# Whose job is the last sum of a batch: one GpSimd addition per batch dropped, and its two terms added by VectorE in PSUM

## The reference

```python
u  = causal_conv4(xc) + conv_b            # (512 tokens, 512 channels)
dt = clip(sigmoid(u @ dt_w.T + dt_b), 1e-4, 1.0)
Bm, Cm = u @ B_w.T, u @ C_w.T             # (512 tokens, 16 states)
for t in tokens:                          # a scan over the tokens
    state = exp(clip(dt[t] * A, -5, 5)) * state + dt[t] * Bm[t] * u[t] + 1e-6
    y[t]  = sum(state * Cm[t], over the 16 states) + D * u[t]
out = (y * silu(z)) @ out_w.T
```

## Time and profile before

| | before |
|---|---|
| median of 3 runs | 1909.05 us (1909.0 to 1915.85) |
| the profiled execution's own time | 1916.34 us |
| its span | 1914.3 us |
| state-space layer with its scans | from about 570 to 1625 us of the span |
| busy over the span | PE 83%, DVE 59%, ACT 51%, POOL 54% |
| mean granted TensorE clock | 0.895 of full speed |

### The profile page before, as it was taken

How to read it: one execution, slowest core, us unless ns; L and a number is a source line. 1 busy time by engine, 2 the same in 40 slices (tenths; PEclk the granted TensorE clock), 3 DMA queues, 4 the chain that set the end, 5 groups by cost and what they waited for, 6 DMA issues and landing times.

```text
span 1914.3 us, 21817 instructions
## 1 busy us (share of the span) xinstructions
PE 1580.1 (83%) x6438; PEld 979.1 (51%) x6439; DVE 1131.5 (59%) x1730; ACT 967.6 (51%) x1749; POOL 1032.0 (54%) x354
## 2 busy tenths in 40 slices
PE   2899686999689979889889799799798684807997
PEld 1565663666335545445445455454455453804665
DVE  4665520444517677786786876777867877323443
ACT  1222111333138867777677777677767773102332
POOL 2010024222107978788888788788787897052222
PEclk9999768999899989989899899799899687658999
DMA  9700114211201111011011110111111110522110
GB/s 330 259 0 0 34 52 126 60 57 51 94 12 28 39 28 36 32 30 38 29 33 34 29 38 30 28 39 31 31 34 34 34 34 23 198 75 68 59 58 25
DMA packets 67889, 108.61 MB, mean 57 GB/s; under 512 B 8730, under 2 KB 37279, under 8 KB 67553
## 3 DMA queue, kind: packets, MB, share of 16 engines
q1 hardware_dynamic: 54240, 76.65, 13.1%
q0 software_dynamic: 9344, 27.31, 3.8%
q10 hardware_dynamic: 4224, 3.67, 0.6%
HBM read 80.04 MB, written 29.39 MB: 57 GB/s over the span
## 4 chain that ended last, share of the span: by engine, by line
PE 66%; DVE 11%; issue 10%; ACT 5%; POOL 5%; DMA 1%; ACTq 1%; SPq 1%; DVEq 0%; POOLq 0%
PE ps L1029 13%; PE ps L1248 10%; PE ps L1189 8%; PE ps L1172 7%; PE ps L1353 6%; PE ps L1279 4%; DVE arena L985 4%; PE ps L1054 3%; POOL arena L371 3%; PE ps L1332 3%; PE ps L1224 3%; PE ps L1315 2%; POOL arena L378 2%; DVE ps L933 2%; PE ps L1045 2%
## 5 line engine op out<-in xcount | busy, mean ns | idle before, releaser
L985 DVE TENSOR_TENSOR_SCAN arena<-arena,ps 128x512 f32<-128x512 f32 x512 | 613.1, 1213 | 255.2 <-PE ps L1029 236.5
L371 POOL TENSOR_TENSOR arena<-arena 128x2048 f32<-128x2048 f32 x128 | 580.3, 4540 | 235.8 <-DVE arena L985 235.1
L1029 PE MATMUL ps<-cst,arena 128*128 128x128 f32 x2836 | 481.4, 300 | 171.1 <-DVE arena L985 55.0
L1029 PEld LDWEIGHTS ps<-cst,arena 128*128 128x128 f32 x2836 | 377.5, 155 | 460.8 <-issue 267.0
L558 ACT ACTIVATE arena<-arena,a_neg 128x512 f32<-128x512 f32 x512 | 366.4, 716 | 138.2 <-DVE arena L985 137.2
L569 ACT ACTIVATE arena<-arena,m_bt 128x512 f32<-128x512 f32 x512 | 363.2, 709 | 29.3 <-PE ps L1029 28.0
L378 POOL TENSOR_TENSOR arena<-arena 128x2048 f32<-128x2048 f32 x64 | 290.5, 4539 | 5.0
L1248 PE MATMUL ps<-arena,tapw 128*128 128x512 f32 x512 | 256.7, 614 | 1.6 <-ACT arena L526 0.9
L478 ACT ACTIVATE arena<-ps,b1t 128x128 f32<-128x128 f32 x312 | 89.2, 368 | 167.4 <-PE ps L1029 167.4
L346 POOL DMA_INDIRECT sorted_rows<-x,pos x64 | 62.3, 974 | 199.1 <-DVE tile_e L814 180.1
L1189 PE MATMUL ps<-arena 128*128 x624 | 151.3, 385 | 7.4 <-ACT arena L478 2.9
(11 more groups left out here) (132 smaller groups left out, 1465.2 us busy)
## 6 DMA issues: line engine op xcount, KB each, us to landing
arena<-c_rows SPq DMA_DIRECT2D x128, 256.0 KB, 3.2
arena<-in_W SPq DMA_DIRECT2D x32, 512.0 KB, 10.5
sorted_rows<-arena POOLq DMA_DIRECT2D x2, 5070.0 KB, 36.0
arena<-sorted_rows SPq DMA_DIRECT2D x78, 130.0 KB, 2.1
x<-in_x SPq DMA_DIRECT2D x8, 512.0 KB, 10.6
arena<-in_conv SPq DMA_DIRECT2D x4, 1024.0 KB, 6.3
x<-residual SPq DMA_DIRECT2D x8, 512.0 KB, 7.6
arena<-in_b SPq DMA_DIRECT2D x2, 1024.0 KB, 11.7
```

Of the source, the lines that this page charges most:

```text
L371: g.tensor_tensor(h, h, m_c[i % RC].unsqueeze(1).to_broadcast([P, KI, SEQ]), ALU.mult)\
L985: v.tensor_tensor_scan(out=h[:, k, :], data0=m_a[g % RA], data1=ps[2 + g % 2][:, :], initial=0.0, op0=ALU.mult, op1=ALU.add).then_inc(S("m ...
L1029: return t.transpose(bank, src[:, k * P:(k + 1) * P], ident)
```

## The change

For the last pair of each batch (pairs 7, 15, ..., 63) GpSimd makes the two products and no sum. VectorE adds both states to PSUM itself: first the odd one (`m_ho`), then, after a wait for its own addition (`m_odd`), the even one (`m_he`), since both write the same bank. It does so in slots 8 to 11 of the next batch and not in 12 to 15; the wait is on the products (`m_cp`) in place of the sum. `summed(pair)` gives the count of `m_q` that now stands for a pair. The scans of the second pair of a batch no longer wait for `m_q`, since VectorE itself has read `m_ho` earlier in its queue.

```diff
+def summed(pair):
+    return pair + 1 - (pair + 1) // PAIRS
...
             for pair in range(BATCH * NS // 2):
                 c_product(2 * pair)
                 c_product(2 * pair + 1)
+                if pair % PAIRS == PAIRS - 1:
+                    continue
                 g.wait_ge(S("m_cp"), 2 * pair + 2)
                 g.tensor_tensor(m_he[pair % 3], m_he[pair % 3], m_ho[pair % 2], ALU.add).then_inc(S("m_q"), 1)
...
-                v.wait_ge(S("m_q"), pair + 1)
+                last = pair % PAIRS == PAIRS - 1
+                if last:
+                    v.wait_ge(S("m_cp"), 2 * pair + 2)
+                else:
+                    v.wait_ge(S("m_q"), summed(pair))
...
+                if last:
+                    v.tensor_tensor(ps[4 + k][:, :], ps[4 + k][:, :], m_ho[pair % 2][:, k, :], ALU.add)\
+                        .then_inc(S("m_odd"), 1)
+                    v.wait_ge(S("m_odd"), KI * b + k + 1)
                 v.tensor_tensor(ps[4 + k][:, :], ps[4 + k][:, :], m_he[pair % 3][:, k, :], ALU.add)\
                     .then_inc(S("m_add"), 1)
...
-                if n % 2 and pair >= 2:
-                    v.wait_ge(S("m_q"), pair - 1)
+                if n % 2 and pair >= 2 and (pair - 2) % PAIRS < PAIRS - 1:
+                    v.wait_ge(S("m_q"), summed(pair - 2))
...
                         turn = (SLOTS * b + q) // KI - 5
-                        if turn >= 0 and turn % 2 == 0 and turn // 2 % PAIRS >= PE_PAIRS:
+                        if turn >= 0 and turn % 2 == 0 and PE_PAIRS <= turn // 2 % PAIRS < PAIRS - 1:
                             m_add(turn // 2, q % KI)
+                        if turn > 0 and turn % 2 and (turn + 1) // 2 % PAIRS == PAIRS - 1:
+                            m_add((turn + 1) // 2, q % KI)
...
             def m_nsum(pair, k):
-                t.wait_ge(S("m_q"), pair + 1)
+                t.wait_ge(S("m_q"), summed(pair))
```

## The result

The changed kernel is slower: 1932.39 us median of 5 runs (1927.23 to 1934.84) beside 1912.53 us for the kernel before in the same session (1909.0 to 1915.85), a ratio of 1.0104 with a 95% interval of 1.0081 to 1.0126, or 19.9 us. The sum in the prediction was 12.9 us, and 1932.4 lies just above its range of 1915 to 1930. The profiled execution took 1934.84 us with a span of 1932.8, 18.5 us above that of the kernel before.

What follows compares the result with a forecast made beforehand. Each batch was taken as one chain through VectorE's scans and TensorE, with GpSimd hardly waited for. 12.0 + 2.6 - 1.75 = 12.9 us, added to the median 1909.05, gave 1922 us; own range 1915 to 1930, 8 in 10 for 1911 to 1931.

Steps and rivals of the forecast that it cites:

- The sum in the prediction: Whole kernel: 12.0 us for batches 1 to 6 plus 2.6 for batch 7 less 1.75 in the tail, 12.9 us slower.
- Slots 8 to 16: From scan 8 to scan 16 of a batch: VectorE's added additions make it 15.62 us against 13.61.
- the dependent step: VectorE, slots 8 to 11: the even addition starts 0.69 us after the odd one it waits for, bounds 0.58 and 0.80.
- The hand-over to TensorE in slots 18 to 20: Transposes of slots 18 and 20 wait for VectorE's scans, so scan 16's delay passes into TensorE's queue and every later slot.
- the clock rival: Slots 11 to 20: TensorE's granted clock falls there, 8 us a batch more, 1970 us in all; 9 in 100.
- the missing sum gives nothing in the batches: Inside the batches: GpSimd, without the last pair's sum, waits for VectorE's scans one product later; gain nothing.
- each batch is one chain, and nothing in it runs to a clock of its own: Whole batch: a delay of scan 16 passes through slots 18 and 20 into every later slot.
- the 2.0 us: Batches 1 to 6: scan 16 and the rest of the batch come 2.0 us later each, 12.0 us together.
- a scatter of up to 4 us around the sum: Seven batches: distances of 132.56 and 133.56 us, mixed in another share, move the time by up to 4 us.
- the tail: End of the last batch: from GpSimd's last product to the finals 5.2 us in place of 6.95, a gain of 1.75.
- all of batch 7's delay reaches this product: Last batch: the full 2.6 us reach GpSimd's product at 1566.59, which waited 1.01 us for a scan.

Runs made afterwards that it cites:

- pool_only: The changed kernel without the odd addition of each batch's last pair, the even one in slots 12 to 15: 1907.49 us beside 1914.49 for the kernel before.
- thrice: The kernel before and the changed one, transposes made three times over in slots 0 to 7 and 50 to 63: 1952.06 and 1961.18 us.
- split: The changed kernel with the even addition moved back to slots 12 to 15, the odd one in 8 to 11: 1938.23 us beside 1914.49 for the kernel before.
- the pads: The kernel before plus one (256, 400 columns) or two linked (220, 320) PSUM multiplications in each of slots 8 to 11: ratios 1.0016, 1.0062, 1.0088, 1.0087.
- pad2x320: The kernel before plus two linked 320-column VectorE multiplications on PSUM in each of slots 8 to 11, batches 1 to 7: ratio 1.0087.
- pad256: The kernel before plus one 256-column VectorE multiplication on PSUM in each of slots 8 to 11, batches 1 to 7: ratio 1.0016.
- dve_only: The kernel before, all GpSimd sums kept, VectorE adding the odd state and then the sum, linked, in slots 8 to 11: 1923.0 us beside 1914.49.
- delay1: The kernel before plus one 8-column SBUF-to-SBUF VectorE operation behind the scan in each of slots 8 to 11, batches 1 to 7: ratio 1.0259.
- delay3: The kernel before plus three linked 8-column SBUF-to-SBUF VectorE operations behind the scan in each of slots 8 to 11, batches 1 to 7: ratio 1.0474.

## Why the prediction was right and wrong

*Right: where the time goes and how much it is there.* Slots 8 to 16 were forecast at 15.62 us and took 15.61 in each batch (that it fits to a hundredth is luck: 9.78 for 9.72 up to slot 12, 5.83 for 5.90 behind it); the dependent step was 0.70 us for the 0.69 taken from the earlier trace rows. The rule of the Trainium skill ("VectorE: DVE Perf Modes", "The DRAIN you can't avoid"), by which the step would have been 0.58, did not hold for it. The hand-over to TensorE in slots 18 to 20 came as in the earlier trace rows, slots 16 to 48 took the same 65.5 us, and the granted clock stayed at 1.00 in slots 8 to 19 (1121.6 to 1142.0), which rules out the clock rival in the place that it named:

```profile
1121.60:1142.00 20.40, 17.87 (x73) 8.98 (x71) 20.16 (x24) 15.09 (x25) 17.88 (x5) 1.00 0.09 27
```

*Right: the missing sum gives nothing in the batches.* `pool_only` shows it, 133.0 us a batch with or without the sum.

*Wrong: "each batch is one chain, and nothing in it runs to a clock of its own".* The step that failed is the one that passed the 2.0 us on one to one. The chain goes through slots 48 to 8, where TensorE idles often and the granted clock falls and rises several times. The falls and rises did not keep their places in the batch. In the changed kernel the clock fell in slots 52, 58 and 63 after batch 1 and in slots 55 and 3 after batch 3. Whether it is low under the z matmuls or under waits then differs, and with it what the same work costs: 1.99 or 3.50 us for the four in the rows above. I had the sign of this in the earlier trace rows (132.56, then 133.56) and in the earlier trace rows, and booked it as a scatter of up to 4 us around the sum. In the profiled pair it was +4.5 us in the six stretches. The whole miss there is 5.6 us (18.5 for 12.9): these 4.5, 1.1 ahead of them, 2.2 after the finals and -2.2 in the tail; the 1.1 and the 2.2 lie within what such parts vary by. That the clock goes with it is in the rows above, and that it is the cause rests on the `thrice` stretches at 1.00, with the limit named there. That the amount is not proportional to the added time is shown by `split` and the pads: with 1.3 us more per batch in slots 8 to 16 the whole time was 1.0117, with 2.6 it was 1.0087. Their intervals overlap, but one to one the second would have lost twice what the first did.

*Mis-sized: the tail.* Forecast for batch 7 from slot 16 on: -1.75 us. It was -3.9. The last product was over at 1629.84, after which the four blocks took 5.4 us, near the forecast 5.2:

```profile
1629.88 0.70 DVE L945 TENSOR_TENSOR ps<-ps,arena 128x512 f32<-128x512 f32 x1 [2.85 <-POOL arena L376]
...
1635.21 2.47 DVE L958 SCALAR_TENSOR_TENSOR arena<-ps,arena 128x512 f32<-128x512 f32 x4
```

The surplus of 2 us came ahead of that, between slot 16 and the last product: slots 16 to 48 of batch 7 took 53.5 us in place of 55.7. The same stretch before and after:

```profile
1522.17:1577.83 55.66, 45.36 (x190) 29.17 (x189) 41.53 (x41) 40.75 (x64) 53.15 (x13) 0.81 0.13 38
```
```profile
1542.35:1595.85 53.50, 43.80 (x193) 28.83 (x191) 41.41 (x42) 41.03 (x65) 51.37 (x12) 0.86 0.12 36
```

The granted clock is higher after, and TensorE is busy 1.6 us less. The product that waited 1.01 us for a scan at 1566.59 before had no such wait after: its counterpart came 18.0 us later, where scan 16 came 20.2 later. So the prediction's step by which all of batch 7's delay reaches this product failed by those 2 us. No run tests this by itself, but kernels with all their sums spread as widely here (`pad2x320` 52.9 us, `pad256` 55.8), so it needs nothing of the change.

*Not forecast:* 2.2 us after the finals, in work that is the same in both. One of them is the wait for the first half of the output projection (5.43 us before, 6.39 after; the granted clock in the 21.1 us from the finals on was 0.74 before and 0.66 after). The other I have not followed; it is within the spread of that part over all kernels.

*The base.* The three runs shown before had their median at 1909.05; in later sessions the same kernel had medians of 1911 to 1915, so some 3 us of the miss in the absolute time are the base and not the change. The difference of 19.9 us against 12.9 stands all the same.

## What to carry to other kernels

Where a loop has a stretch in which TensorE idles and its granted clock falls, the length of a turn is not the sum of its path. Added or saved time shifts the falls against the work, and can settle into a fixed bad rhythm. In the profiled executions here 2.3 us a batch cost 0.9 (`dve_only`), 2.6 cost 2.2 (`pad2x320`) and 1.3 cost 3.6 (`split`). Look at the granted clock stretch by stretch before passing a delay on one to one, and widen the range by the number of turns times the spread between turns. Additions that VectorE takes over belong where it waits: the same two additions cost 1% in slots 8 to 11, and with one of them in slots 0 to 3 the kernel was 0.16% faster than the one before [0.04%, 0.28%].

## What the hardware showed that was not expected

A VectorE operation of 8 columns from SBUF to SBUF (f32, `tensor_scalar`) took 0.14 us while GpSimd was idle and 2.6 to 4.1 us while GpSimd ran a two-input operation of 4.5 us (`delay1`); three in a row took 0.55 us beside an idle GpSimd and up to 7.15 us across the ends of two of its operations (`delay3`). 28 of them, four per batch, cost the kernel 2.6%. VectorE's scans and additions, which have one operand in PSUM, showed nothing of the kind (1.21 and 0.67 us beside a busy or an idle GpSimd), nor did the same `tensor_scalar` on PSUM (0.41 us for 256 columns). And the clock of TensorE, where its falls repeated, did so exactly: `split` had stretches of 56.14 to 56.15 us at a granted 0.79 after five consecutive batches.
